# Query squares summed by one-column matmuls into a score bank, and the output units' halves exchanged

## What is computed

```python
xn = layernorm(x)                                   # 1024 x 512
q, k, v = xn @ Wq.T, xn @ Wk.T, xn @ Wv.T           # 32, 8 and 8 heads of 128
q = q / sqrt(mean(q * q, over the head's 128) + eps) * q_norm_w
k = k / sqrt(mean(k * k, over the head's 128) + eps) * k_norm_w
s = q @ k.T / sqrt(128) + slope[head] * (pos_k - pos_q)      # masked above the diagonal
attn = softmax(s) @ v ; s_out = attn @ Wo.T
g = silu((silu(xn @ gate) * (xn @ up)) @ down)      # weights dequantised from 4 bits
out = x + s_out * g
```

## Time and profile before

| | |
|---|---|
| time, median of 3 runs | 1294.43 us (1294.23 to 1294.84) |
| the profiled execution's own time | 1294.79 us |
| its span, first to last instruction | 1293.0 us |
| PE busy | 1277.0 us, 99% of the span |
| DVE busy | 970.9 us, 75% |
| POOL busy | 702.7 us, 54% |
| ACT busy | 647.8 us, 50% |
| PE idle by the profile | 16.0 us |

### The profile page before, as it was taken

One profiled execution on the slowest core, in us unless ns is written; L12 is line 12 of the kernel. 1 busy time (PEld: TensorE's weight loads), 2 busy tenths in 40 slices (PEclk: granted clock), 3 DMA queues, 4 the chain that ended last, 5 costly groups with the idle time before them and its releaser, 6 DMA issues.

```text
span 1293.0 us, 21088 instructions
## 1 busy us (share of the span) xinstructions
PE 1277.0 (99%) x7141; PEld 1099.1 (85%) x7141; DVE 970.9 (75%) x2089; ACT 647.8 (50%) x1433; POOL 702.7 (54%) x758
## 2 busy tenths in 40 slices
PE   8999999999999999999999999999999999999998
PEld 7888888888888888888888888888888888888886
DVE  6555555578888777877787778777877787778887
ACT  4322222365565555555555555555555555555552
POOL 4855555545555455545554555455545554555486
PEclk9999999999999999999999999999999999999999
DMA  6555444120010000000000010000000000000211
GB/s 195 160 140 130 129 128 130 28 78 17 17 34 17 17 18 33 18 17 17 33 18 17 17 33 17 17 17 34 17 17 18 33 17 18 17 17 17 99 57 66
DMA packets 31965, 62.08 MB, mean 48 GB/s; under 512 B 3840, under 2 KB 4096, under 8 KB 31744
## 3 DMA queue, kind: packets, MB, share of 16 engines
q1 hardware_dynamic: 31872, 60.88, 16.3%
HBM read 56.67 MB, written 4.19 MB: 47 GB/s over the span
## 4 chain that ended last, share of the span: by engine, by line
PE 87%; DVE 8%; ACT 2%; issue 2%; POOL 1%; DMA 0%; SPq 0%; DVEq 0%; POOLq 0%
PE O L1103 31%; PE O L1166 13%; PE S L1692 12%; PE T L1124 8%; PE S L1145 4%; PE S L1148 4%; PE S L1146 4%; DVE pb L845 2%; DVE pb L854 2%; PE T L1708 1%; PE O L1708 1%; PE T L1707 1%; PE O L1707 1%; ACT pb L584 1%; PE O L1706 1%
## 5 line engine op out<-in xcount | busy, mean ns | idle before, releaser
L442 POOL TENSOR_TENSOR pb<-rel,coef 128x1024 f32<-128x1024 f32 (+7 forms) x256 | 292.7, 1158 | 144.1 <-PE T L1124 139.3
L584 ACT ACTIVATE pb<-pb,low 128x1024 f32<-128x1024 f32 (+7 forms) x256 | 198.8, 777 | 189.5 <-DVE low L845 187.6
L829 DVE TENSOR_TENSOR pt_l<-T,pt_h 128x512 fp32r<-128x512 f32 (+3 forms) x384 | 209.9, 550 | 42.3 <-ACT pt_h L574 42.3
L574 ACT ACTIVATE pt_h<-T 128x512 fp32r<-128x512 f32 (+3 forms) x384 | 182.1, 486 | 112.8 <-PE T L1124 110.8
L845 DVE CUSTOM_DVE_ANT_0 pb<-S,pb,ninv 128x1024 f32<-128x1024 f32 (+7 forms) x256 | 207.5, 811 | 34.7 <-PE S L1148 29.8
L1124 PE MATMUL T<-ident,pb 128*128 128x128 f32 x1152 | 183.3, 273 | 4.2 <-DVE pb L854 2.4
L854 DVE TENSOR_SCALAR pb<-pb,rinv 128x1024 f32<-128x1024 f32 (+7 forms) x256 | 172.3, 673 | 9.0
L1124 PEld LDWEIGHTS T<-ident,pb 128*128 128x128 f32 x1152 | 140.1, 140 | 37.2 <-DVE pb L854 6.6
L1145 PE MATMUL S<-kT_h,q_h 128*128 128x512 f32 (+2 forms) x384 | 141.5, 368 | 0.1
L1166 PE MATMUL O<-pt_h,v_h 128*128 128x512 f32 (+2 forms) x384 | 140.8, 367 | 0.1
L1166 PE MATMUL O<-pt_h,v_l 128*128 128x512 f32 (+2 forms) x384 | 133.5, 348 | 0.0
(11 more groups left out here) (181 smaller groups left out, 2901.1 us busy)
## 6 DMA issues: line engine op xcount, KB each, us to landing
wq_in<-in_wq SPq DMA_DIRECT2D x32, 256.0 KB, 2.9
wo_in<-in_wo SPq DMA_DIRECT2D x32, 256.0 KB, 2.5
stage<-in_wkv SPq DMA_DIRECT2D x8, 512.0 KB, 4.5
pb<-in_gate_w SPq DMA_DIRECT2D x14, 256.0 KB, 2.6
pb<-in_gate_z SPq DMA_DIRECT2D x14, 256.0 KB, 3.7
pb<-in_gate_s SPq DMA_DIRECT2D x14, 256.0 KB, 5.1
pb<-in_up_w SPq DMA_DIRECT2D x14, 256.0 KB, 5.3
pb<-in_up_z SPq DMA_DIRECT2D x14, 256.0 KB, 6.2
```

The source lines that it names most:

```text
L442: g_.tensor_tensor(pbuf(idx, t), rel[:, TOK - w:TOK], coef[:, t:t + 1].to_broadcast([P, w]), ALU.mult).then_inc(bias_ready, 1)
L574: a_.activation(pt_lot(pt_h, t, n), bank[:, 0:m * P].rearrange("p (k w) -> p k w", w=P), ACT.Copy).then_inc(tr_hi, 1)
L584: a_.activation(pbuf(idx, t), pbuf(idx, t), ACT.Exp, bias=low[:, idx:idx + 1], scale=-1.0, accum_out=rsum[:, idx:idx + 1]).then_inc(exps_r ...
L829: v_.tensor_tensor(pt_lot(pt_l, t, n), bank[:, 0:m * P].rearrange("p (k w) -> p k w", w=P), f(pt_lot(pt_h, t, n)), ALU.subtract).then_inc( ...
```

## The change

Both halves of the squares of the heads 1 to 31 are now summed on PE: four plain matmuls per half, each with a 128x128 block of `sq` as its stationary operand and the column `cst[:, 2:3]` (128 times -1, float32) as the moving one, so that a block's result is one column of 128 negative sums. Half 0 goes to columns 0 to 3 of `S[0]`, half 1 to columns 512 to 515 of `S[0]`. DVE makes `ms` of them in one instruction on 128x4 elements, where it had a sum over 128x512 elements and an addition on 128x4. The part `"ss1"` of the bank `T` is gone. `scores` of idx 0 and 2, and the transposes of k, wait for the means, since they write to `S[0]`. Head 0 keeps its two sets of four transposes.

The halves of the units are exchanged: j = 0 and j = 2 take c = 1, which reads the `v1` of the head before, and j = 1 and j = 3 take c = 0. The order of POOL's bases, and the halves in which x and g are laid out for them, follow. On DVE, at a group's first head, `q_lo` of `qc0` moves behind `logits` 1, `normalise` 0 and the mean of half 0. In the last head the late unit (`w3_2`) moves from behind `scores` 6 to behind `scores` 4 on PE, and ACT and DVE take tile 4's `exp` or `normalise` ahead of its first lot.

```diff
-PARTS = LOTS[:LOTS.index((3, 0))] + ["ss1"] + LOTS[LOTS.index((3, 0)):]
...
+    SQ1_BANK = S[0][:, CH:TOK]
     SQ_BANK = S[0][:, 0:CH]
...
-    BASES = [0, 2, 4, 1, 3, 5, 7, 6]
+    BASES = [1, 3, 5, 7, 0, 2, 4, 6]
...
         def mean_sq0(h):
             cs = slice(0, CT)
             dve.wait_ge(sq_tr, h)
-            v_.tensor_reduce(out=ssum[:, cs], in_=SQ_BANK.rearrange("p (k w) -> p k w", w=P),
-                             axis=mybir.AxisListType.X, op=ALU.add).then_inc(sq_sum, 1)
-            dve.wait_ge(sq_sum, h)
-            v_.tensor_scalar(ms[:, cs], ssum[:, cs], HD * RMS_EPS, None, ALU.add).then_inc(ms_ready, 1)
+            v_.tensor_scalar(ms[:, cs], SQ_BANK[:, 0:CT], -1.0, HD * RMS_EPS, ALU.mult, ALU.add).then_inc(ms_ready, 1)
+
+        def mean_sq1(h):
+            cs = slice(CT, QT)
+            dve.wait_ge(sq1_tr, h)
+            v_.tensor_scalar(ms[:, cs], SQ1_BANK[:, 0:CT], -1.0, HD * RMS_EPS, ALU.mult, ALU.add).then_inc(ms_ready, 1)
...
                 elif prev:
                     logits(h, 0)
-                    q_lo(at, f"qc0_{j}")
                     logits(h, 1)
                     normalise(h, 0)
                 if prev and (j == 0 or kind == "steady"):
                     mean_sq0(h)
+                if prev and j == 0:
+                    q_lo(at, f"qc0_{j}")
                 normalise(h, 1)
...
-                    project(at, f"w0_{j}", 0 + j % 2, kind == "first")
+                    project(at, f"w0_{j}", 1 - j % 2, kind == "first")
...
             if not (isinstance(h, int) and h == 0 and idx < 2):
                 pe.wait_ge(logits_ready, h * QT + (idx - 1))
+            if idx == 0 and h > 0:
+                pe.wait_ge(ms_ready, 2 * h + 1)
             if idx == 2 and h > 0:
-                pe.wait_ge(sq_sum, h)
+                pe.wait_ge(ms_ready, 2 * h + 2)
...
             pe.wait_ge(out_hi, at.hi(f"qc0_{j}"))
             pe.wait_ge(logits_ready, h * QT + 1)
             for k in range(CT):
-                ins = nc.tensor.transpose(SQ_BANK[:, k * P:(k + 1) * P], sq[:, k * P:(k + 1) * P], ident[:, :])
+                ins = mm(SQ_BANK[:, k:k + 1], sq[:, k * P:(k + 1) * P], cst[:, 2:3], start=True, stop=True)
             ins.then_inc(sq_tr, 1)
+
+        def squares_of_half_1(at, h, nx):
+            pe.wait_ge(out_hi, at.hi(f"qc1_{nx}"))
+            pe.wait_ge(logits_ready, h * QT + 3)
+            for k in range(CT):
+                ins = mm(SQ1_BANK[:, k:k + 1], sq[:, CH + k * P:CH + (k + 1) * P], cst[:, 2:3], start=True, stop=True)
+            ins.then_inc(sq1_tr, 1)
...
                     if kind == "first" and j < 2:
                         return
-                    project(at, f"w{n}_{j}", 2 * n + j % 2, h - 2 - j % 2, 0 if j >= 2 else 2,
-                            at.n(f"v0_{j - j % 2}"))
+                    if j % 2:
+                        outputs = at.n(f"v0_{j - 1}")
+                    else:
+                        outputs = at.n("v1_1") if j else at.n("qc0_0", more=-1)
+                    project(at, f"w{n}_{j}", 2 * n + 1 - j % 2, h - 2 - j % 2, 0 if j >= 2 else 2, outputs)
...
                 scores(h, 4)
+                if not more:
+                    w_unit(3, h - 1, j - 1, late=True)
                 lot(h, 4, 0)
...
                 def squares1(h=h, nx=nx):
-                    squares(at.hi(f"qc1_{nx}"), 1, part_no(h, "ss1"), T[part_bank(part_no(h, "ss1"))])
+                    squares_of_half_1(at, h, nx)
...
-                if not more:
-                    w_unit(3, h - 1, j - 1, late=True)
                 lots(h, 3)
```

More of the change, by code:

```diff
@@ L86 @@
 LOTS = [(t, n) for t in TILES for n in range(len(parts(t)))]
-PARTS = LOTS[:LOTS.index((3, 0))] + ["ss1"] + LOTS[LOTS.index((3, 0)):]
 LN_PARTS = QT + 2
-def place_in_head(h, key):
-    i = PARTS.index(key)
-    return i - 1 if isinstance(h, int) and h == HEADS - 1 and i > PARTS.index("ss1") else i
 def part_no(h, key):
-    return LN_PARTS + len(PARTS) * h + place_in_head(h, key)
+    return LN_PARTS + len(LOTS) * h + LOTS.index(key)
 def part_bank(part):
@@ L254, in attention @@
     tr_ready, tr_hi, tr_lo = sem("tr_ready"), sem("tr_hi"), sem("tr_lo")
-    sq_tr, sq_sum = sem("sq_tr"), sem("sq_sum")
+    sq_tr = sem("sq_tr")
+    sq1_tr = sem("sq1_tr")
     out_ready, out_hi, out_free = keep["out_ready"], sem("out_hi"), keep["out_free"]
@@ L287, in x_part @@
     def x_part(unit):
-        return x_late[unit % NC][:, unit // NC, :]
+        return x_late[1 - unit % NC][:, unit // NC, :]
     def y_part(unit):
-        slot = unit % NC * KT + unit // NC
+        slot = (1 - unit % NC) * KT + unit // NC
         tile, n = (keep["stage"], slot) if slot < 6 else (sq, slot - 6)
@@ L499, in base @@
             n = BASES.index(u)
-            pool.wait_ge(out_free, Places("last", GROUPS - 1).n(f"w{m}_{2 + c}"))
+            pool.wait_ge(out_free, Places("last", GROUPS - 1).n(f"w{m}_{3 - c}"))
             g_.tensor_tensor(part(sT, u), part(sT, u), y_part(u), ALU.mult).then_inc(base_ready, 1)
@@ L732, in group @@
                     q_hi(at, f"qc1_{(j + 1) % PER}")
-                lot(h, 4, 0)
-                exp(h, 4)
+                if more:
+                    lot(h, 4, 0)
+                    exp(h, 4)
+                else:
+                    exp(h, 4)
+                    lot(h, 4, 0)
                 lot(h, 4, 1)
@@ L1002, in group @@
                 if w:
-                    project(at, f"w1_{j}", 2 + j % 2, kind == "first")
+                    project(at, f"w1_{j}", 3 - j % 2, kind == "first")
                 if prev:
@@ L1015, in group @@
                 elif w:
-                    project(at, f"w2_{j}", 4 + j % 2, kind == "first")
-                lot(h, 4, 0)
-                normalise(h, 4)
+                    project(at, f"w2_{j}", 5 - j % 2, kind == "first")
+                    project(at, "w3_2", 7)
+                if more:
+                    lot(h, 4, 0)
+                    normalise(h, 4)
+                else:
+                    normalise(h, 4)
+                    lot(h, 4, 0)
                 if w and more and kind == "steady":
-                    project(at, f"w2_{j}", 4 + j % 2)
+                    project(at, f"w2_{j}", 5 - j % 2)
                 lot(h, 4, 1)
                 if w and more and kind != "steady":
-                    project(at, f"w2_{j}", 4 + j % 2, kind == "first")
+                    project(at, f"w2_{j}", 5 - j % 2, kind == "first")
                 logits(h, 5)
@@ L1041, in group @@
                 if w and not (last and j == 2):
-                    project(at, f"w3_{j}", 6 + j % 2, kind == "first")
+                    project(at, f"w3_{j}", 7 - j % 2, kind == "first")
                 logits(h, 7)
@@ L1327, in group @@
                 pe.wait_ge(logits_ready, g * (PER * QT) - 1)
+                pe.wait_ge(ms_ready, 2 * g * PER + 1)
                 k_transposes(range(0, CT))
```

10 lines of the change are left out of this document (5 added, 5 removed).

## The result

The changed kernel takes 1309.2 us (median of 4 runs, 1308.92 to 1309.46), the kernel before 1294.45 (1294.23 to 1294.84): **1.0114 times as long, interval 1.0102 to 1.0125**, slower by 14.8 us. The profiled execution took 1309.46 us.

The account below looks back on a forecast made before the run. PE, busy for 99% of the span, was taken as the bound. The profiled 1294.8 us plus 27 for the squares less 12.3 of stalls made 1309.5, less 0.36 to the median: 1309 us, range 1283 to 1322.

Parts of the forecast that it names:

- The price of the squares: On PE, eight weight loads of 0.11 us make 0.88 us a set, 0.44 more than before; 62 sets, +27 us.
- Rival 1: Loads of `sq` keep the transposes' pace or hide: 0.48 us a set, 1284 us, faster; chance 0.19.
- rival 3: Column matmuls and loads don't overlap fully: at 0.15 us a load, 1.2 us a set, +47, 1329 us; chance 0.06.
- Rival 4: Four loads for each matmul, or loads twice as long: 1.76 us a set, +82, 1364 us; chance 0.03.
- The stalls: PE's waits for DVE at several places go by the edits of the order, together -12.3 us.
- DVE is not the bound, so I cost it at nothing: About 0.6 us less DVE work in each of 62 places was given no gain of its own.
- tile 7's lots: At j = 0, PE's 0.46 us wait for `normalise` 0 goes with `q_lo` moved behind it; 7 groups, -3.2 us.
- `w0_0` and `w0_2`: Output units no longer read what `v_lo` is making, so their stalls go: -2.7 and -4.7 us.
- head 1: The squares, and the lot behind them, no longer wait for the bank `T`: -0.9 us.
- the last head's late unit: Moved ahead of a lot that waited 0.8 us, the unit (1.4 us of matmuls) removes that wait: -0.8 us.
- rival 2: Stalls stay because something else comes late at the same places; a third of the gain left, 1317 us; chance 0.10.
- The predicted signs: What the profile would show: load pace, set and group lengths, no PE idle at named places, DVE's busy time down 37 us.

Follow-up runs that it names:

- e3_fp32r: The full change with the squares as fp32r and two equal fp32r columns of -1 as moving operand: 1286.02 us, 0.9934 of the kernel before.
- e4_twice: The full change with each set of column matmuls issued twice: 1361.78 us, 1.0519 of the kernel before.
- g2_q_lo_back: The full change with `q_lo` of a group's first head put back between the two logits: 1308.93 us, 1.0111 of the kernel before.
- f3_transposes_twice: The kernel before with each set of four transposes of the squares issued twice, DVE's work unchanged: 1316.25 us, 1.0168 of the kernel before.
- g1_fp32r_q_lo_moved: The kernel before with fp32r column squares and `q_lo` moved behind the mean, nothing else of the order: 1287.33 us, 0.9943 of the kernel before.
- e2_squares_alone: The kernel before with the float32 column squares in the score bank and their waits, its order unchanged: 1309.17 us, 1.0112 of the kernel before.
- f2_fp32r_order_before: The kernel before with the squares as two fp32r columns in the score bank, its order unchanged: 1288.08 us, 0.9951 of the kernel before.
- e1_transposes: The full change with the squares transposed and summed by DVE again, in the score bank: 1293.64 us, 0.9992 of the kernel before.
- f4_fp32r_last_head_back: The full change with fp32r column squares, and the last head alone in the order of before: 1287.58 us, 0.9948 of the kernel before.

## Why the prediction was right, and where it was not

**The price of the squares: right, in mechanism and size.** Eight loads at 0.11 us, 0.88 a set, +27 us, were predicted; it is 0.112, 0.894 and +28.2. That the number of pairs of load and matmul is the price is shown by halving it (`e3_fp32r`, 0.448 a set) and doubling it (`e4_twice`, 1.78 a set, +52.6 us). No run has the loads without their matmuls; that it is the loads is read from the traces, by the 0.03 us that are enough between the first two matmuls of a set, where the others are 0.112 apart with their loads. The choice between the earlier trace rows was by the kind of matmul, and that was the right ground: the same tile `sq`, loaded for transposes, keeps 0.06 (before, in head 1: two loads in 0.20 us, where one lasts 0.14), and loaded for a matmul takes 0.11:

```profile
309.99 0.20 PEld L1188 LDWEIGHTS T<-ident,sq 128*128 128x128 f32 x2 [0.51 <-issue]
```

Rival 1 (loads as cheap as the transposes') falls with it, and rival 3 (loads that don't overlap). Rival 4 too: here one float32 matmul left two loads and two matmuls, and cost twice an fp32r one (0.894 to 0.448 us a set), not four times. The Trainium skill's page "FP8 and Floating Point Precision", section TensorE Precision Notes, gives true FP32 four passes; read as four loads, this trace doesn't agree. The Trainium skill's page "TensorE: Matmul & The Clock Gate", section LDWEIGHTS, gives columns / 1.2 GHz for a load, an estimate of 107 ns for 128 columns; the trace's 112 is near it.

**The stalls: right in sum (13.6 us gone, 12.3 predicted), wrong in what removes them.** The places named were the right ones, and all four stalls of a steady group are gone, among them the short one at its start that I had left in place (0.2 us). The step that failed is "DVE is not the bound, so I cost it at nothing", and with it the list that gave each stall to one edit of the order:

- tile 7's lots, 3.2 us for `q_lo`'s move: gone in the full change without that move (`g2_q_lo_back`), and by longer sets alone (`f3_transposes_twice`). The move does remove this stall when the sets are cheap (`g1_fp32r_q_lo_moved`).
- `w0_0` and `w0_2`, 7.4 us for the exchange: mostly gone without it, by DVE's lighter load. The stalls ahead of output units of 512 columns sum to some 7.8 us before, to 1.4 in `e2_squares_alone` and to 2.4 in `f2_fp32r_order_before`. The exchange removes them too when DVE is heavy (`e1_transposes`), but there the time comes back elsewhere. In the full change it is worth 2 us.
- head 1, 0.9 us: two thirds came. The squares no longer wait, but the lot behind them does, 0.36 us in the full change (at 310.89), now for `normalise`, which had been hidden behind the wait for the bank; with cheap sets (`f2_fp32r_order_before`) it is 0.80 us and next to nothing is gained.
- the last head's late unit, -0.8 us: not by this stall. The wait of 0.75 us became one of 1.43 at the next lots; `e2_squares_alone`, with the order of before in that head, keeps 0.75. But `f4_fp32r_last_head_back`, which undoes this edit alone, is 1.0 to 1.6 us slower, since a unit then waits in the epilogue; what the edit is worth by itself stays open.

By the runs, one way to add it up is this. Relief is worth 7.6 us (`e1_transposes` to `e3_fp32r`), cover by the dear sets 4.5 (`e3_fp32r` to the full change, 27.7 paid and 23.2 seen), the order 1 us (`e1_transposes`, within the noise): 13.1 of the 13.6. They are not independent, and another way gives other parts: relief 6.4 in the order of before (`f2_fp32r_order_before`), the order 2.1 with cheap sets (`f2_fp32r_order_before` to `e3_fp32r`) and nothing behind the dear ones (`e2_squares_alone`).

So the number 1309 came out of a price that was understood and a gain whose size was right by the list of stalls, for other reasons than those given. That last is luck: the edits that I paid 12.3 us for add nothing to the squares alone. Had DVE's work not been cut, the same working would have said -12 where `e1_transposes` shows -1: rival 2, stalls that stay since something else comes late at the same places, is what that kernel shows.

**The predicted signs.** Two records of load and matmul for a column, 0.11 us apart: seen. A steady group of 132.3 us: the second matmul behind its first set comes at 650.98 and in the next group 132.16 us later, without idle time. No idle time at `w0` and at tile 7's lots: seen. DVE's busy time down by 37 us: it is 42. No new wait for `q_lo`, `normalise` 1 or a mean: none in the full change, but the waits for the mean are there in `e1_transposes`, where DVE still sums.

**A version that beats both.** `e3_fp32r` takes 1286.0 us, 8.4 less than the kernel before and 23.2 less than the change: the column sum is worth having when its matmul is issued once. It pays with squares that are rounded to fp32r.

## What to carry to other kernels

Before a reduction moves to TensorE, count the weight loads of the compiled program and not the matmuls of the source: with next to nothing to stream, loads times 0.11 us was the price here, and a float32 matmul had two. A transpose's load took half of that, but its 128 columns took 0.11 us all the same. An engine with idle time and off most of the chain can still be worth several us when the bound engine stops for it in many short places; list those stalls from start to start, since 0.16 us of each hides behind a record. And give a stall to an edit only after undoing that edit: here two or three edits each removed the same stall, and one edit alone merely moved it to the next place.

## What was not expected of the hardware

- The second matmul behind a set of columns starts 0.20 us after the first (650.78 and 650.98), where 0.12 is usual for 256 columns; this is 0.08 us of each set's 0.894, and it is there with fp32r columns too (642.37 and 642.58). It isn't owed to the columns: behind the transposes of the earlier trace rows the first matmul starts at 627.51 and the second at 627.72, and so in all 55 sets (0.20 us by the median).

```profile
627.51 0.37 PE L1103 MATMUL O<-w_h,xh 128*128 128x256 f32 x1
```

- The loads of float32 columns and of fp32r columns keep one pace, 0.112 us; float32 costs more by their number alone.
- Transposes of float32 run at 0.109 us each, 0.44 a set, though their loads can follow each other in 0.06 us: so their loads don't set that pace. The two happen to lie so near that a set of four fp32r columns (0.448) costs PE what four transposes cost (0.440).
